# Sixteen experts run as eight pairs, each expert's rows cut into 32-row tiles on TensorE's column quadrants

## The reference, cut to what matters

```python
logits = xf @ gate_w.T                       # 512 tokens, 16 experts
probs = jax.nn.sigmoid(logits)
top_vals, sel = jax.lax.top_k(probs, 2)
weights = top_vals / (top_vals.sum(-1, keepdims=True) + 1e-06)
...                                          # rank of each token in its expert; 80 places per expert
padded = jnp.zeros((sentinel + 1, d), xf.dtype).at[slot].set(x_rep)
padded = padded[:sentinel].reshape(E, capacity, d)          # 16 x 80 x 512
h = jax.nn.gelu(jnp.einsum('ecd,edf->ecf', padded, w1), approximate=False)      # 16 x 80 x 1024
out_padded = jnp.einsum('ecf,efd->ecd', h, w2).reshape(sentinel, d)
gathered = out_padded[jnp.minimum(slot, sentinel - 1)]
out = (gathered * weights.reshape(-1)[:, None]).reshape(T, K, d).sum(axis=1)
```

## Time and profile before

| | us |
|---|---|
| median of three runs | 1198.41 |
| lowest and highest | 1194.51, 1200.53 |
| the profiled execution | 1192.27 |
| its span | 1190.5 |
| expert stage in it, first row transpose to last down matmul | 936.1 to 1175.5 |

### The profile page before, as it was taken

The page is one execution under the profiler, slowest core; times in us unless marked ns, Lnnn a source line. Parts: engine busy times, 40 slices in busy tenths (PEclk is TensorE's granted clock), DMA queues, the critical chain, the costliest instruction groups (busy, mean ns, idle before and its releaser), DMA issues.

```text
span 1190.5 us, 7210 instructions
## 1 busy us (share of the span) xinstructions
PE 816.6 (69%) x2318; PEld 366.0 (31%) x2318; DVE 430.9 (36%) x1318; ACT 323.0 (27%) x604; POOL 241.6 (20%) x94
## 2 busy tenths in 40 slices
PE   4725365636562651586976999288765599999995
PEld 2202132213121410342433444143524233333332
DVE  3774445443545257406663000601933000000003
ACT  1344706461746165410001100012501111111110
POOL 1038414841484048400000000000000200000002
PEclk9657566757575755597997999689975799999998
DMA  9600006000500040175000030300030657788883
GB/s 318 253 1 18 0 0 221 18 0 4 217 18 0 3 174 18 18 238 212 1 0 1 0 141 0 141 1 0 2 141 5 221 198 297 296 295 310 292 294 115
DMA packets 62839, 133.42 MB, mean 112 GB/s; under 512 B 7712, under 2 KB 17312, under 8 KB 62288
## 3 DMA queue, kind: packets, MB, share of 16 engines
q1 hardware_dynamic: 59440, 124.20, 29.1%
q0 software_dynamic: 1920, 6.29, 1.8%
q10 hardware_dynamic: 1440, 2.46, 0.6%
HBM read 122.35 MB, written 8.49 MB: 110 GB/s over the span
## 4 chain that ended last, share of the span: by engine, by line
PE 55%; DVE 17%; ACT 16%; DMA 5%; issue 4%; POOL 2%; SPq 0%; DVEq 0%; POOLq 0%
PE PS L1188 8%; PE PS L1211 8%; PE PS L1066 5%; PE PS L1072 5%; PE PS L950 5%; PE PS L1036 4%; PE PS L970 4%; PE PS L920 3%; DVE AR L707 3%; PE PS L936 3%; ACT AR L481 3%; DMA AR<-in_w 3%; PE PS L1088 2%; ACT AR L507 2%; ACT L477 2%
## 5 line engine op out<-in xcount | busy, mean ns | idle before, releaser
L950 PE MATMUL PS<-AR,QT 32*128 32x512 f32 x128 | 102.1, 939 | 115.9 <-ACT AR L468 113.1
L1188 PE MATMUL PS<-AR 128*80 128x512 f32 x256 | 113.2, 595 | 1.9 <-DMA AR<-in_w 1.9
L1211 PE MATMUL PS<-AR 128*80 128x512 f32 x256 | 112.5, 592 | 0.7 <-DVE AR L903 0.7
L920 PE MATMUL PS<-CST,AR 128*128 128x128 f32 (+1 forms) x348 | 52.7, 305 | 77.3 <-DVE AR L637 31.9
L903 DVE COPY AR<-PS 128x320 f32<-128x320 f32 x32 | 14.2, 487 | 228.8 <-PE PS L920 228.8
L988 PE MATMUL PS<-AR 128*128 128x256 f32 x64 | 30.0, 649 | 96.1 <-POOL AR L411 68.5
L672 DVE MAX8 AR<-AR 128x8 f32<-128x64 f32 x512 | 66.9, 210 | 60.2 <-ACT AR L468 56.1
L361 POOL TENSOR_TENSOR RS<-VE,CST 128x4 f32<-128x4 f32 x6 | 6.1, 1021 | 395.5 <-DVE VE L634 395.5
L707 DVE SCALAR_TENSOR_TENSOR AR<-AR,TH 128x2048 f32<-128x2048 f32 x16 | 38.1, 2379 | 121.7 <-ACT AR L481 121.7
L950 PEld LDWEIGHTS PS<-AR,QT 32*128 32x128 f32 x128 | 31.5, 271 | 158.7 <-ACT AR L468 136.8
L920 PEld LDWEIGHTS PS<-CST,AR 128*128 128x128 f32 (+1 forms) x348 | 44.7, 165 | 100.6 <-issue 65.2
(11 more groups left out here) (227 smaller groups left out, 1167.7 us busy)
## 6 DMA issues: line engine op xcount, KB each, us to landing
AR<-in_w SPq DMA_DIRECT2D x32, 2048.0 KB, 9.5
AR<-in_ctxT SPq DMA_DIRECT2D x16, 768.0 KB, 11.8
AR<-in_ctx SPq DMA_DIRECT2D x16, 768.0 KB, 8.3
AR<-in_W SPq DMA_DIRECT2D x2, 4096.0 KB, 28.4
token_rows<-AR SPq DMA_DIRECT2D x1, 2560.0 KB, 14.9
AR<-token_rows SPq DMA_DIRECT2D x5, 512.0 KB, 6.4
expert_rows<-AR ACTq DMA_DIRECT2D x15, 160.0 KB, 6.2
AR<-AR POOLq DMA_DIRECT2D x8, 256.0 KB, 3.4
```

The source lines that it names most:

```text
L920: return eng.transpose(dst, src, c("ident", rows)[:, 0:rows])
L950: mm(PS[:, 4 + k % 2, :], QT[r, b * T:(b + 1) * T], KT[r, cols], start=True, stop=False)
L1188: last = mm(PS[0:CAP, 4 + j, :], XET[:, k, e * CAP:(e + 1) * CAP], EW1[e % 2][:, k, 512 * j:512 * j + 512], start=k == 0, stop=k == KD - 1)
L1211: last = mm(PS[0:CAP, e % 2, :], HT[e % 2][:, f, :], EW2[e % 2][:, f, :], start=f == 0, stop=f == F // P - 1)
```

## The change

The 16 experts become eight pairs (`NPAIR`). The 80 rows of an expert are 64 (`ROWS`) and a rest of 16 (`TAIL`).

- **Up of a pair.** Stationary tiles are 128 x 32. Quadrants 0 and 1 hold rows 0 to 31 and 32 to 63 of the first expert, 2 and 3 those of the second; each quadrant's matmul has its own moving slice of 512 columns of its expert's `w1`. Two halves of 512 columns by four k: 32 matmuls. A third pass covers rows 64 to 95 (of which 16 count): quadrant 0 the first expert's columns 0 to 511, quadrant 1 its columns 512 to 1023, quadrants 2 and 3 those of the second: 16 matmuls, into bank 6.
- **Down of a pair.** 32 matmuls with 512 moving columns for the 64 rows, and 32 with 256 moving columns for the rest.
- **Transposes.** `H` of a pair is 128 rows, and its tail `HTL` 128 rows: 12 transposes of 128 x 128 in three groups of four. They share two banks (3 and 7) in turn with `row_columns`, whose copies move from ScalarE to VectorE; one counter `tg_sb` counts the groups copied, and group g waits for copy g-2.
- **Weights.** Three slots `EW` of 4 MB instead of four halves of 4 MB in pairs: half s of the stream is both experts' `w1` (s even) or both experts' `w2` (s odd) of pair s // 2, and goes to slot s % 3. Halves 0, 1 and 2 are loaded ahead of the stage; then half 3 waits for up of pair 0, half 4 for down of pair 0, half 5 for up of pair 1, half 6 for down of pair 1, and so on.
- **ScalarE** does three Gelus of 128 partitions per pair, two copies of the result (512 and 256 columns) and six stores per pair instead of two.
- **One-hot of the last pair.** `OHL` becomes three arrays; VectorE writes them with 24 small operations, two memsets and eight operations that select the weights, each behind the one before. TensorE transposes them behind the first two row chunks.
- **End.** Two experts instead of one stay out of DRAM: 12 matmuls (per token block one of 512 columns and two of 256) instead of four. The gather waits for the stores of pair 6.

The diff, cut to its core:

```diff
@@ -32,6 +32,9 @@
...
+NPAIR, ROWS, TAIL = E // 2, 64, CAP - 64
+XCH = [min((2 * CAP * (m + 1) + TAIL - 1) // P + 1, NXC) for m in range(NPAIR)] + [NXC]
+GRP = [5 + 3 * m + XCH[m] - XCH[0] for m in range(NPAIR + 1)]
...
@@ -221,15 +225,19 @@
...
-        XET = at(21504, KD, NSLOT)
-        Y = [at(26624, D), at(27136, D)]
...
+        XET = at(8192, KD, NSLOT + TAIL)
+        EW = [at(0, 2, KD * F), at(29696, 2, KD * F), at(21504, 2, KD * F)]
+        EW1 = [w.rearrange("p a (k n) -> p a k n", k=KD) for w in EW]
+        EW2 = [w.rearrange("p a (k n) -> p a k n", k=F // P) for w in EW]
...
-        EW1 = [at(0, KD, F), at(29696, KD, F)]
-        EW2 = [at(4096, F // P, D), at(33792, F // P, D)]
...
@@ -325,27 +333,31 @@
...
+            def load_half(s):
+                m, down = divmod(s, 2)
+                for x in range(2):
+                    if down:
+                        load(EW2[s % 3][:, x, :, :], w2v[2 * m + x], f"ld_e{s % 3}")
+                    else:
+                        load(EW1[s % 3][:, x, :, :], w1v[2 * m + x], f"ld_e{s % 3}")
...
-            load_w1(0)
-            load_w2(0)
+            load_half(0)
             eng.wait_ge(S_["av_ps"], 4)
-            load_w1(1)
-            load_w2(1)
+            load_half(1)
+            eng.wait_ge(S_["o_ps"], B)
+            load_half(2)
...
-            for e in range(2, E):
-                eng.wait_ge(S_["m1_ps"], e - 1)
-                load_w1(e)
-                eng.wait_ge(S_["m2_ps"], e - 1)
-                load_w2(e)
+            for s in range(3, 2 * NPAIR):
+                m, down = divmod(s - 3, 2)
+                if down:
+                    eng.wait_ge(S_["m2_ps"], m + 1)
+                else:
+                    eng.wait_ge(S_["m1_ps"], m + 1)
+                load_half(s)
...
@@ -589,33 +602,34 @@
...
+            def pair_gelu(m):
+
+                eng.wait_ge(S_["m1_ps"], m + 1)
+                if m:
+                    eng.wait_ge(S_["ht_ps"], 3 * m)
+                eng.activation(H[:, 0:512], PS[:, 4, :], ACT.Gelu).then_inc(S_["h_sb"], 1)
+                eng.activation(H[:, 512:1024], PS[:, 5, :], ACT.Gelu).then_inc(S_["h_sb"], 1)
+                eng.activation(HTL, PS[:, 6, :], ACT.Gelu).then_inc(S_["h_sb"], 1)
...
+                    for x in range(2):
+                        r = (2 * m + x) * CAP
+                        eng.dma_start(yrows[r:r + ROWS, :], y[ROWS * x:ROWS * x + ROWS, :]).then_inc(S_[st], 16)
+                        for n in range(2):
+                            q = ROWS * x + 32 * n
+                            eng.dma_start(yrows[r + ROWS:r + CAP, 256 * n:256 * n + 256], yt[q:q + TAIL, :])\
+                               .then_inc(S_[st], 16)
...
@@ -887,21 +901,42 @@
...
+            link(eng.memset(OHT[1], 0.0))
+            for b in range(B):
+                for x in range(2):
+                    rank, w = RT[:, b, E - 2 + x:E - 1 + x], LS[:, b, x:x + 1]
+                    link(ts(OHM[:, b, ROWS * x:ROWS * x + ROWS], c("slot")[:, 0:ROWS], rank, w, ALU.is_equal, mul))
+                    for n in range(2):
+                        q = ROWS * x + 32 * n
+                        link(ts(OHT[n][:, b, q:q + TAIL], c("slot")[:, ROWS:CAP], rank, w, ALU.is_equal, mul))
+            link(eng.memset(XET[:, :, NSLOT:NSLOT + TAIL], 0.0))
+            eng.memset(EV3[:, :], 0.0).then_inc(S_["ohl"], 1)
...
@@ -1161,60 +1196,84 @@
...
+            def pair_up(m):
+
+                w, a = EW1[2 * m % 3], 2 * m * CAP
+                eng.wait_ge(S_[f"ld_e{2 * m % 3}"], 32 * (2 * m // 3 + 1))
+                eng.wait_ge(S_["tg_sb"], GRP[m] - 3 if m else 2)
+                if m:
+                    eng.wait_ge(S_["h_sb"], 3 * m)
                 for j in range(2):
                     for k in range(KD):
-                        last = mm(PS[0:CAP, 4 + j, :], XET[:, k, e * CAP:(e + 1) * CAP],
-                                  EW1[e % 2][:, k, 512 * j:512 * j + 512], start=k == 0, stop=k == KD - 1)
+                        for q in range(4):
+                            x, at_ = q // 2, a + CAP * (q // 2) + 32 * (q % 2)
+                            mm(PS[32 * q:32 * q + 32, 4 + j, :], XET[:, k, at_:at_ + 32],
+                               w[:, x, k, 512 * j:512 * j + 512], start=k == 0, stop=k == KD - 1)
+                for k in range(KD):
+                    for q in range(4):
+                        x, j, at_ = q // 2, q % 2, a + CAP * (q // 2) + ROWS
+                        last = mm(PS[32 * q:32 * q + 32, 6, :], XET[:, k, at_:at_ + 32],
+                                  w[:, x, k, 512 * j:512 * j + 512], start=k == 0, stop=k == KD - 1)
                 last.then_inc(S_["m1_ps"], 1)
 
...
+            def pair_down(m):
+
+                w, s = EW2[(2 * m + 1) % 3], 2 * m + 1
+                eng.wait_ge(S_[f"ld_e{s % 3}"], 32 * (s // 3 + 1))
+                eng.wait_ge(S_["tg_sb"], GRP[m + 1])
+                if m:
+                    eng.wait_ge(S_["y_sb"], 2 * m)
+                for f in range(F // P):
+                    for q in range(4):
+                        mm(PS[32 * q:32 * q + 32, m % 2, :], HT[:, f, 32 * q:32 * q + 32], w[:, q // 2, f, :],
+                           start=f == 0, stop=f == F // P - 1)
+                for f in range(F // P):
+                    for q in range(4):
+                        x, n = q // 2, q % 2
+                        at_ = ROWS * x + 32 * (f // 4)
+                        last = mm(PS[32 * q:32 * q + 32, 2, 0:256], HTT[:, f % 4, at_:at_ + 32],
+                                  w[:, x, f, 256 * n:256 * n + 256], start=f == 0, stop=f == F // P - 1)
+                last.then_inc(S_["m2_ps"], 1)
...
+            eng.wait_ge(S_["ohl"], 1)
+            for n, src in enumerate((OHM, OHT[0], OHT[1])):
+                eng.wait_ge(S_["tg_sb"], n + 1)
+                for b in range(B):
+                    last = tr(PS[:, (3, 7)[n % 2], b * P:(b + 1) * P], src[:, b, :])
+                last.then_inc(S_["ow_ps"], 1)
...
+                for n in range(XCH[m], XCH[m + 1]):
+                    row_columns(n, GRP[m] + n - XCH[m])
+                eng.wait_ge(S_["h_sb"], 3 * (m + 1))
+                for j in range(3):
+                    g = GRP[m + 1] - 3 + j
+                    eng.wait_ge(S_["tg_sb"], g - 1)
                     for f in range(4):
-                        k = 4 * j + f
-                        last = tr(PS[:, 6 + j, f * CAP:(f + 1) * CAP], H[e % 2][0:CAP, k * P:(k + 1) * P], rows=CAP)
+                        src = H[:, (4 * j + f) * P:(4 * j + f + 1) * P] if j < 2 else HTL[:, f * P:(f + 1) * P]
+                        last = tr(PS[:, (3, 7)[g % 2], f * P:(f + 1) * P], src)
                     last.then_inc(S_["ht_ps"], 1)
...
+                if m + 1 < NPAIR:
+                    pair_up(m + 1)
+                pair_down(m)
+            eng.wait_ge(S_["y_sb"], 2 * NPAIR)
+            for b in range(B):
+                t, bank = slice(b * T, (b + 1) * T), (4, 5, 3, 7)[b]
+                mm(PS[:, bank, :], OWM[:, t], Y[(NPAIR - 1) % 2], start=True, stop=False)
+                mm(PS[:, bank, 0:256], OWT[0][:, t], YT[(NPAIR - 1) % 2], start=False, stop=False)
+                mm(PS[:, bank, 256:512], OWT[1][:, t], YT[(NPAIR - 1) % 2], start=False, stop=True)\
+                    .then_inc(S_["last_ps"], 1)
```

More of the change, by code:

```diff
@@ L167, in build @@
         LW = sb("LW", [P, B, 2])
+        LS = sb("LS", [P, B, 2])
         IDB = sb("IDB", [P, P], bf16)
@@ L591, in _ @@
                            ACT.Sigmoid).then_inc(S_["probs"], 1)
[L592 to L618, removed]
@@ new lines, in pair_gelu @@
+            def pair_gelu(m):
[5 more added lines that the diff above has]
+                eng.activation(HTL, PS[:, 6, :], ACT.Gelu).then_inc(S_["h_sb"], 1)
+            pair_gelu(0)
+            for m in range(NPAIR):
+                if m + 1 < NPAIR:
+                    pair_gelu(m + 1)
+                y, yt, st = Y[m % 2], YT[m % 2], f"st_y{m % 2}"
+                eng.wait_ge(S_["m2_ps"], m + 1)
+                if m >= 2:
+                    eng.wait_ge(S_[st], 16 * 6 * (m // 2))
+                eng.activation(y, PS[:, m % 2, :], ACT.Copy).then_inc(S_["y_sb"], 1)
+                eng.activation(yt, PS[:, 2, 0:256], ACT.Copy).then_inc(S_["y_sb"], 1)
+                if m + 1 < NPAIR:
+                    eng.wait_ge(S_["y_sb"], 2 * (m + 1))
+                    for x in range(2):
[5 more added lines that the diff above has]
+                               .then_inc(S_[st], 16)
@@ L896, in _ @@
[L896 to L904, removed]
+            for x in range(2):
+                link(ts(LW[:, :, :], I8F[:, :, :], float(E - 2 + x), None, ALU.is_equal))
+                link(tt(LW[:, :, :], LW[:, :, :], WT2[:, :, :], mul))
+                link(tt(LS[:, :, x], LW[:, :, 0], LW[:, :, 1], add))
+                link(tt(WT2[:, :, :], WT2[:, :, :], LW[:, :, :], sub))
@@ new lines, in _ @@
+            link(eng.memset(OHT[0], 0.0))
```

(40 more changed lines are left out.)

51 lines of the change are left out of this document (18 added, 33 removed).

## The result

| | before | after |
|---|---|---|
| median of the runs, us | 1196.46 | 1234.69 |
| lowest, highest | 1191.50, 1200.53 | 1232.92, 1237.81 |
| span of the profiled execution | 1190.5 | 1231.1 |
| first row transpose to the end of the last down | 239.5 | 280.6 |

The changed kernel is slower: the ratio to the kernel before is 1.034, 95% interval 1.030 to 1.037. The forecast was 1232 us, its range 1217 to 1263.

A forecast was written before the change was run, and what follows sets the result against it. TensorE was taken to bound the stage, weight stream close behind. Quadrants save 55 us, eaten by six waits (72 us), clock (13), head and end (about 4); timeline 33.4 us later, 1198.4 + 33.4 = 1232 us, range 1217 to 1263.

The forecast's parts named there:

- What bounds the kernel: Expert stage of the kernel before: TensorE bound, busy 235.6 of 239.5 us, with the weight stream close behind.
- the quadrants: Up and down of a pair: four quadrant matmuls take 0.86 us like one; 20.6 us a pair, 55 us saved.
- The rival that each group pays its own exit: Quadrant matmuls of a pair: 0.2 us exit for each of 28 groups, 45 us more, 1277 us; overlap rival's chance 8%.
- the 1.12 us per group: Quadrant matmuls at the page's 3.07x: 6.2 us more per pair, 50 us in all, 1282 us; within the 8% overlap rival.
- The weight stream: Up(2) to up(7): load issued when the preceding down ends, landing after 14.1 us; TensorE idles about 12 us each time.
- The clock: Start of each up behind a wait: granted clock halves after the idle time, costing 2.1 us (1.5 to 2.8).
- The period: From the end of down(m) to that of down(m+1): 37.2 us, six times; two experts before took 28.6 us.
- The head: Before up(0): five transpose groups delay it 2.1 us; VectorE's longer chain, some 7 us more, ends near 931, hidden.
- The end: After the last down: gather (1218.6) and matmuls (1219.1) finish about equal; last additions end at 1221.1 instead of 1187.7.
- The sum: Whole kernel: 33.4 us later, 1226 us for a profiled execution, 1232 us against the median; chance 82%.

The follow-up runs named there:

- use-order run: The changed kernel with weight-stream halves taking slots in the order TensorE uses them, so the load of up(m+2) waits for up(m); 1153.2 us, ratio 0.965.

## Why the prediction was right

**What bounds the kernel, and the quadrants.** Eight groups of four quadrant matmuls take 6.87 us in the down, exactly what eight single matmuls took the earlier trace rows; the third pass takes 3.43 us for four groups, the tail of the down 3.45 to 3.51 us for eight of half length. In the use-order run a pair is 7.00 + 3.43 + 6.87 + 3.45 = 20.75 us without waits, where 20.6 were forecast from the earlier trace rows. The rival that each group pays its own exit is out, since one of its groups would take 1.06 us and not 0.86. Four quadrants here do four times the work of one matmul in the same time, also in a long run.

That also rules out the 1.12 us per group worked out from the Trainium skill (TensorE: Matmul & The Clock Gate, Part 3). The 3.07x there is for four row tiles, while the quadrants here are column tiles. A single group with its exit would be 4 x 0.86 / 1.06 = 3.2x, an estimate from the earlier trace rows; whether the page's figure counts the exit in this way, no run here shows.

**The weight stream.** Six waits were forecast near 12 us each; six came, 71.7 us in all, from up(2) to up(7), at the line named. Issue to landing was 14.5, 15.0, 15.2, 14.2, 14.3 and 14.3 us in the six periods (in the chain, 0.37 us of SP plus the load), 14.6 on average, where 14.1 was taken. TensorE worked 2.6 us of it on transposes (978.69 to 981.27), where 1.9 were taken, and idled 12.0 us on average.

**The clock.** The first part of the six ups took 9.86, 9.27, 8.84, 9.15, 9.22 and 9.31 us, 9.28 on average; at full clock it is 7.00. So 2.3 us where 2.1 was taken. That it is the clock was shown by the run that keeps it up: its six periods are 14.7 us shorter, of which the six first parts are 13.3, for an expected 14. At the medians it was worth 9.8 us; in its profile the end, with the stalls of the last down, gives 4.9 us back.

**The period.** 38.3, 38.1, 38.0, 37.2, 37.5 and 37.5 us, on average 37.8 against 37.2. The load took 0.5 us more than taken, the clock 0.2, the matmuls 0.2, and the hand-overs 0.3 less. Over six that is 3.4 us of the miss.

**The head.** Up(0) starts 5.0 us after the first transposes instead of 1.9: 3.1 us later, forecast 2.1, and its 96 records took 11.2 instead of 10.3 us, as part of them ran at the low clock. The rows of the head (VectorE, SP, TensorE):

```profile
933.96 0.31 DVE L914 TENSOR_SCALAR KP<-CST,RT,LS 128x64 f32<-128x64 f32 x1
...
935.19 0.06 DVE L919 MEMSET EV<- 128x1 f32 x1
937.97 1.97 PE L955 MATMUL PS<-CST,AR 128*128 128x128 f32 x8 [18.90 <-DMA AR<-token_rows]
...
942.88 7.78 PE L1219 MATMUL PS<-AR 128*32 128x512 f32 x64
```

VectorE's chain of small operations ended at 935.2, not at 931. Of these 4 us, 1.9 are the later start of everything; the rest was mis-sized: the list grew by 9.8 us instead of 7. Its 24 small operations, chained, stand 0.35 us apart on average, where four unchained ones of the kernel before took 0.27 each, and the two memsets 0.65 us. It stayed 2.7 us ahead of the rows, so the cover held, with less to spare than I said.

**The end.** From the end of the last down to the end of the last addition 9.8 us (1218.6 to 1228.4), forecast 9.9. The six stores were issued at 0.44 to 0.60 us each, 2.7 us, not 2.1.

**The sum.** The profiled span grew by 40.6 us, forecast 33.4. The difference of 7.2 us is 1.9 ahead of the stage, 1.0 + 0.9 in the head, 3.4 in the periods, and the rest cancels. The medians differ by 38.2 us. The mechanism and its place were right, and most terms came out a little larger than taken. That the median missed by only 2.7 us (1234.7 for 1232) is partly luck. The forecast added the 6.1 us by which the profiled execution of the kernel before lay below its median, and for the changed kernel this distance was 1.8 us.

## What to carry to other kernels

When a buffer ring feeds work that is software-pipelined, number its slots in the order in which the engine uses the data, not in the order of the data: with three slots in data order the next load waited for the work right in front of its user. Read from the list of loads which instruction each wait names, and from the engine's list how much work lies between that instruction and the user of the load; here 2.6 us of work stood against 14.6 us of load, and exchanging the numbers turned 1234.7 into 1153.2 us. An added unit of work that is moved to hide it still costs its own time on the engine that bounds the stage.

## What was not expected of the hardware

- The fourth load of 2 MB taken up by SP in a period held SP: at 980.2 its issue took 9.7 us instead of 0.5 (the row of SP above, 367/507/9746), until 990, after the first of the four had landed at 988.1. In the six periods it was 8.8 to 10.4 us. It cost nothing here, since SP had nothing else to do.
- In the period shown the weight stream ran at 366 to 387 GB/s under the quadrant matmuls and at 398 with TensorE idle. The quadrants by themselves are no limit at that level: in the use-order run it ran at 402 and 418 GB/s from 984 to 988 and from 988 to 992, with TensorE busy all the time on quadrant matmuls, and at 302 from 996 to 1000. What sets the rate from stretch to stretch wasn't tried; the two stretches compared above also load different weights.
- The quickest loads of 0.25 MB landed 2.4 to 2.7 us after their issue, where the first of two loads of 2 MB took 7.8 to 9.4: an eighth of the bytes takes about three tenths of the time.
- In three of the five profiles of quadrant kernels the last down took 4.7 to 5.8 us longer than the others, in pauses of up to 0.8 us for which the profile shows no wait, at a granted clock of 1.00. GpSimd issues its gathers meanwhile, but it does so in the two profiles without the pauses too. The cause stays open.
- The unchanged part ahead of the stage ended anywhere between 933.8 and 942.0 us in the profiled executions, so stages are better compared from their own first instruction.
